# Attention scores in blocks of four tokens instead of eight, eight array tiles, and a program without loops

## The reference, cut to what matters

```python
# block 1: linear attention over the HEADS of one token, then an MLP
xn = ln(q_x, ln1_w, ln1_b)
q, k, v = xn @ wq + bq, xn @ wk + bk, xn @ wv + bv        # 16 heads of 16 features
fq, fk = elu(q) + 1, elu(k) + 1
kv  = einsum('bhnd,bhne->bnde', fk, v)                    # sum over the heads of token n
qkv = einsum('bhnd,bnde->bhne', fq, kv)
attn = qkv / (einsum('bhnd,bnd->bhn', fq, fk.sum(heads)) + 1e-6)
x = q_x + attn @ wo + bo
x = x + gelu(ln(x, ln2_w, ln2_b) @ fc_w + fc_b) @ proj_w + proj_b
# block 2: two of eight experts per sequence
gates = softmax over the top 2 of (x.mean(tokens) @ gate_w.T + gate_b)
out = sum over experts e of gates[e] * gelu(x @ expert_w[e].T + expert_b[e])
```

## Time and profile before

| | us |
|---|---|
| median of 3 runs | 1176.44 |
| lowest, highest | 1176.12, 1178.38 |
| the profiled execution | 1176.61 |
| its span (first to last instruction) | 1174.8 |
| mean granted clock of TensorE | 0.927 |

### The profile page before, as it was taken

The page is one execution under the profiler, slowest core; times in us unless marked ns, Lnnn a source line. Parts: engine busy times, 40 slices in busy tenths (PEclk is TensorE's granted clock), DMA queues, the critical chain, the costliest instruction groups (busy, mean ns, idle before and its releaser), DMA issues.

```text
span 1174.8 us, 23424 instructions
## 1 busy us (share of the span) xinstructions
PE 1047.1 (89%) x8136; PEld 780.8 (66%) x8136; DVE 730.5 (62%) x1692; ACT 498.5 (42%) x771; POOL 178.1 (15%) x113
## 2 busy tenths in 40 slices
PE   5767989989898899999998899999999899897766
PEld 3354858677676768686867668686868576666533
DVE  2286656666666677676766676767767675745323
ACT  1313443535353444636463354545463444242322
POOL 1011011111121110212121210202021111111000
PEclk9857998989898999999998899999999999897979
DMA  4535352434344435454543435354545434131113
GB/s 175 137 80 135 79 124 67 105 88 97 96 98 108 91 82 140 104 138 103 127 114 92 107 89 127 94 137 103 138 103 140 113 83 98 37 81 54 37 41 121
DMA packets 255834, 119.93 MB, mean 102 GB/s; under 512 B 225169, under 2 KB 241809, under 8 KB 255505
## 3 DMA queue, kind: packets, MB, share of 16 engines
q1 hardware_dynamic: 249104, 108.47, 37.2%
q10 hardware_dynamic: 6656, 10.50, 2.5%
HBM read 60.20 MB, written 58.72 MB: 101 GB/s over the span
## 4 chain that ended last, share of the span: by engine, by line
PE 75%; issue 13%; DVE 5%; POOL 3%; DMA 1%; ACT 1%; ACTq 0%; DVEq 0%; SPq 0%; POOLq 0%
PE pw L966 16%; PE pj L951 15%; PE ps L927 12%; PE ps L909 7%; PE pw L937 5%; PE pw L877 4%; PE pj L877 4%; PE pw L909 3%; PE ps L1008 2%; PE ps L865 2%; PE pw L865 2%; POOL x_sb L451 1%; PE pj L1052 1%; PE pw L917 1%; DVE hn L621 1%
## 5 line engine op out<-in xcount | busy, mean ns | idle before, releaser
L966 PE MATMUL pw<-hT,w_fc 128*128 128x512 f32 x768 | 212.6, 418 | 3.8 <-issue 3.3
L951 PE MATMUL pj<-w_pj,hidden 128*128 128x256 f32 x1536 | 213.0, 288 | 1.3 <-DVE hidden L698 1.3
L951 PEld LDWEIGHTS pj<-w_pj,hidden 128*128 128x128 f32 x1536 | 191.1, 188 | 22.3 <-issue 15.0
L529 ACT ACTIVATE xhT<-pw,col 128x512 f32<-128x512 f32 x128 | 88.2, 689 | 277.4 <-PE pw L966 276.8
L698 DVE TENSOR_TENSOR hidden<-xhT,hidden 128x512 fp32r<-128x512 f32 x128 | 88.6, 692 | 169.5 <-ACT hidden L530 169.5
L684 DVE TENSOR_TENSOR am<-ps,mask 128x512 f32<-128x512 f32 x256 | 159.0, 685 | 19.6 <-PE ps L927 18.8
L966 PEld LDWEIGHTS pw<-hT,w_fc 128*128 128x128 f32 x768 | 145.0, 200 | 36.4 <-issue 4.6
L927 PE MATMUL ps<-kq 16*128 16x128 f32 x2048 | 146.9, 438 | 9.2 <-DVE am L684 9.2
L927 PEld LDWEIGHTS ps<-kq 16*128 16x128 f32 x2048 | 128.4, 329 | 30.9 <-issue 21.8
L909 PE MATMUL ps<-xhT,w_qkv 128*128 128x512 f32 x256 | 120.6, 626 | 2.5 <-ACT xhT L482 2.5
L536 ACT ACTIVATE ot<-pw,den_eps 128x512 f32<-128x512 f32 x64 | 81.6, 1275 | 50.4 <-PE pw L937 50.4
(11 more groups left out here) (109 smaller groups left out, 1171.7 us busy)
## 6 DMA issues: line engine op xcount, KB each, us to landing
scratch_nd<-ot SPq DMA_DIRECT2D x32, 512.0 KB, 4.1
nd<-scratch_nd SPq DMA_DIRECT2D x96, 128.0 KB, 2.6
x_sb<-in_x SPq DMA_DIRECT2D x16, 512.0 KB, 4.6
scratch_v<-feat_v ACTq DMA_DIRECT2D x16, 512.0 KB, 2.8
scratch_q<-fqk SPq DMA_DIRECT2D x32, 256.0 KB, 2.7
scratch_k<-fqk SPq DMA_DIRECT2D x32, 256.0 KB, 3.1
vd<-scratch_v SPq DMA_DIRECT2D x128, 64.0 KB, 2.6
kq<-scratch_q SPq DMA_DIRECT2D x128, 64.0 KB, 2.5
```

The lines of the kernel that those rows point to most:

```text
L529: nc.scalar.activation(gelub[:, m % 2], pw[n], ACT.Gelu, bias=b_fc[:, m:m + 1])
L951: last = nc.tensor.matmul(pj[u][:, D * s:D * (s + 1)], hidden[:, m % SLOTS, a, lo:lo + P], w_pj[:, b, m], start=(m == 0 and n == 0 and s = ...
L966: last = nc.tensor.matmul(pw[bank], w_fc[:, b, c, P * m:P * (m + 1)], hT[:, a, c], start=(n == 0), stop=(n == len(order) - 1))
```

## The change

A block has four tokens (TB = 2, TA = 4) and 64 rows. A strip j now has two blocks side by side in the array (v = 0, 1), so scores use eight array tiles of 32 rows and 64 columns and weighted uses eight of 64 rows and 32 columns. A tile has two scores stages and two weighted stages, each of 64 matmuls; all 512 columns of the four banks hold squares of 64 x 64. The strides of kd and qd stay at KG = 8 elements. The outputs of weighted go to `sa[0]` and `sa[1]`; ACT copies both, in rounds 1 and 3. A2 moves to the banks sb2, q's matmuls to pw, k's to sa. The copy buffers of elu get a tile of their own. up(m) takes bank m % 2.

DRAM scratch of q and k has runs of 32 tokens instead of 64, and v is loaded by 16 DMAs per tile instead of 8.

D2 becomes DV, DQ and DK. The stages of every iteration are written out in `iterations()`: no loops are left but those for a third expert, all waits are for constants, and SP's `held` is gone. J2, Y, DS, Z and D1 (DVE's statistics and norms) stand between other rounds than before; K0 and K1 stand earlier; in iterations 3 to 6 DK and B0 stand between A2 and H; in iterations 16 and 17 and all early ones H stands behind B0 where there is one; XS, J2, Z, E and G of tile 15 stand among the expert work of tile 11.

```diff
-TB = 4
+TB = 2
 TA = 2 * TB
-GG = QT // TA
-RG = 4
-HG = GG // 2
-ROUNDS = GG // RG
+BLOCK = TA * H
+KG = HALF // (2 * TA)
+ROUNDS = 4
...
-FULL = ["L", "XS", "VL", "M1", "K0", "J2", "Y", "M2", "DS", "M3", "Z", "D1", "K1", "M4", "N0", "XL", "X", "J7", "JA", "YB", "E", "VT", "N", "D2", "A2",
-        "F1", "R", "F3", "F4", "SA", "H", "B0", "FX", "F2"]
+TAIL = ["DV", "DQ", "DK", "A2", "F1", "R", "F3", "F4", "SA", "H", "B0", "FX", "F2"]
+HEAD_TAIL = ["XL", "E", "X", "J7", "JA", "YB", "G", "VT", "N", *TAIL]
+FULL_TAIL = ["XL", "X", "J7", "JA", "YB", "E", "VT", "N", *TAIL]
+MERGED = ["L", "XS", "VL", "K0", "M1", "J2", "Y", "M2", "K1", "DS", "Z", "M3", "D1", "M4", "N0"]
+EARLY = ["L", "VL", "K0", "M1", "Y", "M2", "K1", "DS", "M3", "D1", "M4", "N0", "X", "J7", "JA", "YB", "VT", "N",
+         "DV", "DQ", "A2", "R", "DK", "SA", "B0", "H"]
...
+def iterations():
+
+    yield 0, ["DS:0", "L:1", "D1", "W1", "X", "DV", "DQ", "DK"]
+    yield 1, ["DS", "D1", "VL", "K0", "K1", "X", "DV", "DQ", "DK", "L:2", "WS", "VT", "B0"]
+    yield 2, ["VL", "K0", "DS", "D1", "Y", "B1", "X", "DV", "B2", "K1", "DQ", "B3", "B4", "N0", "VT", "DK", "YB", "N",
+              "A2", "R", "SA", "B0", "H"]
+    yield 3, EARLY
+    for i in range(4, 7):
+        yield i, [
+            s for t in EARLY for s in {"L": ["L", "XS"], "Y": ["J2", "Y"], "M3": ["Z", "M3"], "YB": ["YB", "E"]}.get(t, [t])]
+    for i in range(7, TILES):
+        yield i, MERGED + (HEAD_TAIL if i % PER_BATCH == PER_BATCH - 1 else FULL_TAIL)
+    yield 16, ["XS", "VL", "K0", "M1", "J2", "Y", "M2", "K1", "Z", "M3", "M4", "N0", "XL", "J7", "JA", "YB", "E", "VT", "N",
+               "F1", "F3", "F4", "A2", "R", "SA", "B0", "H", "FX", "F2"]
+    yield 17, ["XS", "M1", "J2", "Y", "M2", "Z", "M3", "M4", "N0", "XL", "J7", "JA", "YB", "E", "N",
+               "F1", "F3", "F4", "A2", "R", "SA", "H", "FX", "F2"]
+    yield 18, ["XS", "C1", "J2", "C2", "Z", "C3", "C4", "XL:11", "J7", "JA", "E", "XS:15", "J2:15", "F1:11", "Z:15", "F3:11",
+               "F4:11", "FX:11", "E:15", "F2:11", "G:15", "XL:12"]
...
-                    src = v_dram.rearrange("(h d) (j b t) -> j b d h t", d=HD, j=NQ, b=2)
+                    src = v_dram.rearrange("(h d) (j b v t) -> j b v d h t", d=HD, j=NQ, b=2, v=2)
                     for j in range(NQ):
                         for b in range(2):
-                            sp.dma_start(vd[2 * j + b::2 * NQ].rearrange("p (h t) -> p h t", h=H), src[j, b]).then_inc(S["v_in"], 16)
+                            for v in range(2):
+                                sp.dma_start(vd[2 * j + b::2 * NQ].rearrange("p (v h t) -> p v h t", v=2, h=H)[:, v],
+                                             src[j, b, v]).then_inc(S["v_in"], 16)
...
+                        if "B" in parts and r % 2 == 0 and u == int(r == 0):
+                            dst = ot[:, :, :].rearrange("p h (b v a k) -> p b v k h a", b=2, v=2, k=KG)
+                            for v in range(2):
+                                wait(f"sa_full{v}", at(f"sa_full{v}", 1))
+                                src = sa[v].rearrange("p (k h a) -> p k h a", k=KG, h=H)
+                                nc.scalar.activation(dst[:, r // 2, v], src, ACT.Identity,
+                                                     bias=den_eps[:, :]).then_inc(S[f"sa_free{v}"], 1)
...
-                def scores(r):
+                def scores(b):
 
                     wait("sc_free", at("sc_free"))
-                    for g in range(RG):
-                        at_g = slice(RG * (r % 2) + g, P * HG, HG)
-                        for j in range(NQ):
-                            rows = slice(32 * j, 32 * j + HD)
-                            last = nc.tensor.matmul(ps[:, j, P * g:P * (g + 1)], kd[rows, r // 2, at_g], qd[rows, r // 2, at_g],
-                                                    start=True, stop=True)
+                    for k in range(KG):
+                        for v in range(2):
+                            for j in range(NQ):
+                                rows = slice(32 * j, 32 * j + HD)
+                                cols = slice(BLOCK * KG * v + k, BLOCK * KG * (v + 1), KG)
+                                last = nc.tensor.matmul(ps[BLOCK * v:BLOCK * (v + 1), j, BLOCK * k:BLOCK * (k + 1)],
+                                                        kd[rows, b, cols], qd[rows, b, cols], start=True, stop=True)
                     last.then_inc(S["sc_full"], 1)
 
-                def weighted(r):
+                def weighted(b):
 
                     wait("sc_free", at("sc_free"))
-                    wait("pw_free0", at("pw_free0", up_in_w))
-                    for g in range(RG):
-                        for j in range(NQ):
-                            last = nc.tensor.matmul(pw[0][32 * j:32 * j + 32, P * g:P * (g + 1)], vb[:, GG * j + RG * r + g],
-                                                    am[:, r % 2, j, P * g:P * (g + 1)], start=True, stop=True)
-                    last.then_inc(S["am_used"], 1)
+                    for k in range(KG):
+                        for v in range(2):
+                            rows = slice(BLOCK * v, BLOCK * (v + 1))
+                            cols = slice(BLOCK * k, BLOCK * (k + 1))
+                            for j in range(NQ):
+                                last = nc.tensor.matmul(sa[v][32 * j:32 * j + 32, cols], vb[rows, KG * (2 * j + b) + k],
+                                                        am[rows, j, cols], start=True, stop=True)
+                            if k == KG - 1:
+                                last.then_inc(S[f"sa_full{v}"], 1)
...
-                        if r == 0:
-                            up(1)
-                    if "B" in parts and r < ROUNDS - 1:
-                        if r + 1 == ROUNDS // 2:
-                            wait("kq_in1", at("kq_in1"))
-                        scores(r + 1)
+                    if "B" in parts and r == 1:
+                        empty("sa")
+                        wait("kq_in1", at("kq_in1"))
+                        scores(1)
                     if "C" in parts and r:
                         wait("rest_ready", at("rest_ready"))
                         down(2 * r - 1)
+                    if "B" in parts and r == 2:
+                        weighted(1)
+                    if "C" in parts:
                         up(2 * r + 1)
-                    if "B" in parts:
-                        weighted(r)
+                    if "B" in parts and r == 0:
+                        empty("sa")
+                        empty("pw")
+                        weighted(0)
```

286 lines of the change are left out of this document (115 added, 171 removed), and 3 rows, old and new, of the table INC.

## The result

The changed kernel takes 1126.8 us (median, 1124.9 to 1129.7) where the kernel before takes 1176.6 beside it: 0.9576 of it, 95% interval 0.955 to 0.960. Faster, but by 50 us where 111 were forecast.

The account below looks back on a forecast made before the run. TensorE was taken as the bound: array tiles 96, SP's queue -11, early iterations 5 and 5, iterations 16 and 17 5, iteration 18 6, loops 5, together 111 us off 1176.4, written 1066 us; range 1042 to 1148.

Parts of the forecast that it names:

- main term: TensorE's scores and weighted stages in eight array tiles: 6.9 instead of 12.9 us per tile, 96 us in 16 tiles.
- the price of SP's longer queue: Eight more vd loads per tile on SP make attnT late: about 1.0 us given back in each of 11 iterations, -11.
- the "Zero" for TensorE's instructions: Fetching TensorE's longer straight program of some 24,500 loads and matmuls costs nothing; bound 0 to 15 us.
- the gain in iteration 2: Iteration 2, stages interleaved with the loads: gain of 5 us, estimated from idle pieces; bounds 0 and 10.
- rivals B: Eight strided streams share the partitions' read capacity, so scores stages take 4.1 us: about 1110 us; chance 0.13.
- C for the scores: A step has fixed length despite half-wide pairs, 0.24 us in scores: 1137 us, or 1148; chance 0.10.
- D: Weighted pairs are bound by issue at 31.6 ns each, so 512 pairs take 16.2 us per tile: 1203 us; chance 0.11.
- rival F: Tiles work as said but the chain behind them becomes the bound, attnT late by 2.1 us: 1098 us; chance 0.12.
- Loops written out: The one jump back with a 3.26 us gap and low clock behind it goes: gain 5 us.
- Iterations 3 to 6: DK and B0 before H remove a 5.54 us gap, leaving some 4.3: order gain 5; 29 us for the whole stretch.
- From iteration 16 on: attnT waits in iterations 16 and 17 go (5), iteration 18's gap before transposes goes (6); whole stretch 21 us.
- VectorE and ScalarE: Mask multiplications fall from 256 to 128 of 685 ns, ot copies stay 64; worth nothing by itself.

Follow-up runs that it names:

- e6: Changed kernel with K0 and K1 behind M4, third-expert branch behind F4, and the scores(1) burst cut in two around down(1): 1081.7 us.
- e3: Changed kernel with K0 and K1 behind M4 (in iteration 2, K1 behind B4), so both nd trips precede them on SP: 1105.2 us.
- e2: The kernel before the change with its loops written out and nothing else: 1166.3 us.
- e16: One of the follow-up runs; the text ties this number to no particular change or measured time.
- e13: Changed kernel with only 8 vd loads per tile (v = 0) issued from iteration 7 on, so half of vd holds older data: 1106.8 us.

## Why the prediction was right in its main term and wrong beside it

The sum gave 111 us and 50 were found. Three of its terms failed: the price of SP's longer queue, the "Zero" for TensorE's instructions, and the gain in iteration 2. In the order in which they were mended, moving K0 and K1 gave back 22 us, moving the branch 17 more, cutting the burst 6: 45 of the 61. Most of what is left lies in the opening, which even in e6 is 18 us longer than forecast.

- **Array tiles, the main term: right.** Scores 2.28 to 2.34 us where 2.44 were forecast, a step of 0.13 us; rivals B, C for the scores and D are out. **The weighted stage was mis-sized**: 1.4 to 1.5 us, not 1.03, because "so the weighted stage is bound by its stream" holds for 32 pairs and not for 128: eight pairs take 0.084 us, not 0.055. 0.4 x 32 stages = 13 us, against 4 that the scores gave back. The Trainium skill (TensorE: Matmul & The Clock Gate, section "Back-to-back issue gap") gives about 25 ns from start to start for matmuls of 64 columns or fewer; measured are 10.5 ns a pair, less than half.
- **SyncE: the mechanism was right, the chosen value wrong.** "I take 0.5 us and keep 0 and 2.9": the second nd write was found 31.8 us after M1 against the bounds 27 and 31.4, so at the pessimistic one; nd write to attnT takes 12.6 us (573.09 to 584.45 + 1.23) as forecast. The vd loads were priced at 0.66 us each and take 0.81. This is rival F, not in each middle iteration but in four of nine (0.6 to 2.6 us each) and in iteration 16 (5.4), and e3 prices it at 22 us.
- **Loops written out, "Zero, bound 0 to 15 us": the zero was wrong.** Writing the loops out gave 10 us by itself (e2), where 5 were summed. But the bursts stop for 12.8 us inside the scores, and the clock falls behind the stops: it was 1.00 in the middle iteration, now 0.97. I had named the case myself ("if instruction fetches stall TensorE in the new bursts") and then priced it by traces with no such burst. TensorE uses 16 KB of instructions (256) in a 2.3 us stage, and a fetch mostly needs 2.2 to 2.8 us from its start until TensorE goes on. The Trainium skill (Runtime: NRT & Kernel Launch, section "Instruction fetch mechanics") calls a crossing of a 16 KiB boundary mostly hidden, since issue is slower than the refill; in these bursts the measurement is otherwise.
- **The branch was no part of the sum.** It wasn't in the diff, so I didn't ask what covers it. From its register load to the next matmul it takes 1.14 us (598.67 to 599.81) and shows 0.65 to 1.1 us in nine iterations since the issue has so little lead there.
- **Iteration 2: wrong sign.** "5, by estimate from its idle pieces; 0 and 10 are the bounds" looked at TensorE's idle pieces and not at SP. With the q stores, K1 and 16 vd loads ahead, the second nd write goes out 9.3 us later and A2 begins 10.5 later. An opening has no slack to hide a longer queue. How much each of the three costs is only in part shown: with K1 behind (e3) the write goes out at 97.6 us and A2 begins at 112.0, 3.7 us sooner.
- **Iterations 3 to 6: right in sum (25.2 for 29)**; the hn wait is gone, the gap behind H's subtraction is 2 us, not 4.3, and the 1.51 us ahead of scores(0), whose banks ScalarE still reads, were overlooked.
- **From iteration 16 on: 21.3 for 21, but in part by luck.** The gap before Z's transposes is gone. The waits for attnT in iterations 16 and 17 are not, as the sum had it: 5.37 and 1.64 us where it was 2.21 and 4.01. What the sum didn't have made up for it: the wait for hn of 5.5 us in iteration 16 fell to 0.4.
- **VectorE and ScalarE: right.** Mask 128 x 683 ns, no new wait on either in the middle.
- **The DMA share**: the packets and their share should have made 52% by their own numbers, not 55; measured are 42.9%. Nothing rests on it. In rival F, 2.9 x 11 was added to a sum that already held 0.5 x 11: 1092 and not 1098.
- Summed: with SP, the branch and half of the bursts mended (e6), iterations 7 to 15 gain 50.3 us, the 50 of the forecast. That they agree so closely is luck as well: the short gain of the weighted stages and the stops that are left stand against a give-back of 9 us that doesn't come once SP is mended. The forecast described a kernel in which nothing else came late.

## What to carry to other kernels

When a stage is made shorter, or is made of more instructions in the same time, list what it was covering: not only waits that the diff names but also branches, register chains, the issue times of other queues and the supply of instructions; in the kernel before they cost nothing and show nowhere. When removing one of two late things gains nothing, look whether the other wait grew by the same amount (34.0 to 45.0 us here) before dismissing it, and test them together. A wait that the profile puts down to issue can be two things: split it by where in the stage it stands before pricing a cure. For bursts of over a hundred small matmuls, spread them, and expect differences of some 20 us between programs that differ only in where they lie in memory.

## What the hardware showed that was not expected

- Instructions come in blocks of 256 (16 KB). From a fetch's start to the matmul that ends a stop 2.2 to 2.8 us pass, with DMA engines idle (e16, 943.2 us) or full alike, and up to 3.7 where the fetch itself is long; from its end 1.2 to 1.7. 128 idle instructions turn a kernel of 1082 us into one of 1117.
- A run of `sem_inc` on TensorE isn't free: 128 of them lengthened an iteration by 13.6 us, 64 by 4.2, although it waited there for 3.9 us anyway.
- In eight array tiles TensorE sustains a load and a matmul every 10.5 ns (weighted, the same to 0.1 ns in most undisturbed stages of the middle) and every 16.3 ns (scores, strided).
- A DMA issue of vd on SP rose from 0.66 to 0.81 us with the split pattern; half as many (e13) still took 0.81 each (8 in 6.47 us).
